# The experts' last step: close() of three of five groups moved from VectorE to GpSimd

## The chip, the cores and the metric

The kernel runs on one core of a Trainium2 chip. Times are device microseconds of one execution of the whole program; the median of 3 runs is 4957.95 us (4957.88 to 4960.18). The profile is of one further execution, taken by the hardware profiler. The core has TensorE (PE, with its weight loads PEld), VectorE (DVE), ScalarE (ACT), GpSimd (POOL) and SyncE (SP), which only issues transfers here. Each engine works through its own queue in order; they meet by semaphores.

## The reference, cut to what matters

A graph layer, a linear attention and a mixture of experts stand one after the other, on 3125 nodes of 256 features, with residuals. Only the last part is touched:

```
def _L0_ffn_ref(x, gate_w, gate_b, w1, b1, w2, b2, gamma, beta):
    gate_logits = x @ gate_w + gate_b
    topk_vals, topk_idx = jax.lax.top_k(gate_logits, K)          # K = 2 of E = 16
    topk_w = jax.nn.softmax(topk_vals, axis=-1)
    h = jax.nn.relu(jnp.einsum('bsh,ehf->bsef', x, w1) + b1)
    expert_out = jnp.einsum('bsef,efh->bseh', h, w2) + b2
    sel = jnp.take_along_axis(expert_out, topk_idx[:, :, :, None], axis=2)
    moe = jnp.sum(topk_w[..., None] * sel, axis=2)
    y = x + moe
    mu = jnp.mean(y, axis=-1, keepdims=True)
    var = jnp.var(y, axis=-1, keepdims=True)
    return (y - mu) / jnp.sqrt(var + EPS) * gamma + beta
...
x = x + _L0_ffn_ref(_layernorm(x, axis=-1)[None], ...)[0]
```

## The kernel before, in words

The program has five stages one behind the other: `prepare` (norm, projections, records of the edges), `pass_one` and `pass_two` (attention over the edges), `finish` (output projection, linear attention, the gate) and `experts`. In the profile `experts` is the last stage. All order within an engine is written out by hand; there is no planner.

In `experts` the 3125 rows stand as 25 blocks (NB) of 128 rows (P) by 256 features (D), and the blocks in five groups of five (G5). Rows sorted by expert go in 66 tiles through the two layers: GpSimd fetches a tile's rows (L2570), TensorE turns and multiplies them, ScalarE applies relu, VectorE adds the second bias (`take`, L2653), GpSimd scatters the result to `back_rows` in DRAM (L2580). While the last scatters run, VectorE adds beta to the residual rows x1 (L2663).

Then comes the end, which the change touches. SP loads the scattered results back, one transfer per group (L2556). For each group g VectorE runs `add_up(g)`: ten scalar_tensor_tensor (L2669), each the sum of xn with a gathered row times its gate weight, then five bn_stats (L2672) and five bn_aggr (L2675). ScalarE takes the square root of the variance (L2603). `scale_of(g)` on VectorE makes reciprocal and shift (L2681, L2682). With these ScalarE writes the normed rows to `second`, five activations (L2606), and raises s_unit. `close(g)` on VectorE multiplies a group of `second` with gamma (L2687) and adds the residual rows x1 (L2688), each one instruction of 128x1280; it raises s_final, on which SP sends the group's rows out (L2561, L2562). In VectorE's queue `close(g - 1)` stands behind `scale_of(g)`, so that ScalarE's activations of a group run beside the next group's sums; the last `close` stands at the end.

`Chain` (`link`) is a helper: an instruction given to it raises a semaphore, and the engine waits for it before it goes on. In the profile's names x1, `second` and the loaded rows are all parts of the tile `big`; gamma, beta, statistics and scales are parts of `WA`.

Of the kernel before, what the change touches and what calls it, by code (L numbers as in the profile page):

```python
# [11 lines left out]
ALU = mybir.AluOpType  # L12
# [6 lines left out]
NB = (N + P - 1) // P  # L19
# [107 lines left out]
def bc(ap, axis, count):  # L127

    shape = list(ap.shape)
    shape.insert(axis, count)  # L130
    return ap.unsqueeze(axis).broadcast_to(shape)


def wait(eng, sem, value):

    if not isinstance(value, int) or value > 0:
        eng.wait_ge(sem, value)
# [1815 lines left out]
G5 = 5  # L1953
# [498 lines left out]
SENT = 3  # L2452
ROWS = 4
FIVES = TOP * NB // G5


def experts(nc, a, dr, kp, sem, out):
# [4 lines left out]
    with ExitStack() as ctx:  # L2462
# [18 lines left out]
        x1, second, W2 = whole(NB, D), whole(NB, D), whole(EXPERTS, FC, D)  # L2481
# [8 lines left out]
        gamma, beta = room(D), room(D)  # L2490
# [19 lines left out]
        s_w = sem("s_w")  # L2510
# [18 lines left out]
        s_unit = sem("s_unit")  # L2529
        s_dve = sem("s_dve")  # L2530
        s_var = sem("s_var")
        s_std = sem("s_std")
        s_final = sem("s_final")
        s_out = sem("s_out")
        block = ctx.enter_context(nc.Block())

        @block.sync
        def _(sp):
            sp.dma_start(b1[:, :], a["L0_ffn_b1"]).then_inc(s_b1, 16)
            sp.dma_start(gamma, a["L0_ffn_gamma"].rearrange("(o e) -> o e", o=1).broadcast_to([P, D])).then_inc(s_w, 16)  # L2540
            sp.dma_start(beta, a["L0_ffn_beta"].rearrange("(o e) -> o e", o=1).broadcast_to([P, D])).then_inc(s_w, 16)
            def load(t):
                i = t % SENT
                e = sp.value_load(tile_ei[0:1, t:t + 1], min_val=0, max_val=EXPERTS - 1)
                wait(sp, s_h, t - SENT + 1)
                sp.dma_start(w1[i], a["L0_ffn_w1"][bass.ds(e, 1), :, :].rearrange("e (c p) f -> p (e c) f", p=P)).then_inc(s_w1[i], 16)
                wait(sp, s_ycopy, t - SENT + 1)
                sp.dma_start(b2row[i], a["L0_ffn_b2"][bass.ds(e, 1), :].broadcast_to([P, D])).then_inc(s_b2[i], 16)

            for t in range(NT):  # L2550
                load(t)
            for i in range(ROWS):
                sp.wait_ge(s_store[i], 16 * len(range(i, NT, ROWS)))
            for g in range(NB // G5):
                rows = back_d[g * G5 * P * TOP:(g + 1) * G5 * P * TOP, :]
                sp.dma_start(back[:, g * G5:(g + 1) * G5, :, :].rearrange("p b c d -> p b (c d)"),  # L2556
                             rows.rearrange("(b p c) d -> p b (c d)", p=P, c=TOP)).then_inc(s_back[g], 16)
            for g in range(NB // G5):
                sp.wait_ge(s_final, g + 1)
                lo, hi = g * G5, min(g * G5 + G5, NB - 1)  # L2560
                sp.dma_start(out[lo * P:hi * P, :].rearrange("(b p) d -> p b d", p=P), second[:, lo:hi, :]).then_inc(s_out, 16)  # L2561
            sp.dma_start(out[(NB - 1) * P:N, :], second[0:LAST, NB - 1, :]).then_inc(s_out, 16)  # L2562
            sp.wait_ge(s_out, 16 * (NB // G5 + 1))

        @block.gpsimd
        def _(pool):
            def fetch(t):
                i = t % ROWS
                wait(pool, s_turned, t - ROWS + 1)
                pool.indirect_dma_start(out=row[i], out_offset=None, in_=x2_d,  # L2570
                                        in_offset=bass.IndirectOffsetOnAxis(ap=come[:, t:t + 1], axis=0)).then_inc(s_row[i], 16)

            pool.wait_ge(s_table, 1)
            for t in range(ROWS):
                fetch(t)
            for t in range(NT):
                if t + ROWS < NT:
                    fetch(t + ROWS)
                pool.wait_ge(s_ycopy, t + 1)
                pool.indirect_dma_start(out=back_d, out_offset=bass.IndirectOffsetOnAxis(ap=go[:, t:t + 1], axis=0),  # L2580
                                        in_=y[t % ROWS], in_offset=None).then_inc(s_store[t % ROWS], 16)

        @block.scalar
        def _(act):
# [25 lines left out]
        def _(dve):  # L2610
            link = Chain(dve, s_dve)
# [10 lines left out]

            for k in range(FIVES):
                u, q = k % 2, slice(k * G5, (k + 1) * G5)
# [10 lines left out]
            link(nc.vector.tensor_scalar(dump, dump, 2.0 * NP + 1, None, ALU.add))  # L2635
            dve.wait_ge(s_slot, FIVES)
            link(nc.vector.tensor_copy(slot, psS[:, 0:NT]))
# [22 lines left out]
                take(t)  # L2660

            dve.wait_ge(s_w, 32)
            link(nc.vector.tensor_tensor(x1, x1, bc(beta, 1, NB), ALU.add))  # L2663

            def add_up(g):
                dve.wait_ge(s_back[g], 16)
                for c in range(TOP):
                    for b in range(g * G5, g * G5 + G5):
                        have = link.post(nc.vector.scalar_tensor_tensor(xn[:, b, :], back[:, b, c, :], share[:, c, b:b + 1], xn[:, b, :], ALU.mult, ALU.add))  # L2669
                    link.until(have)  # L2670
                for i in range(G5):
                    have = link.post(nc.vector.bn_stats(stats[:, i, :], xn[:, g * G5 + i, :]))  # L2672
                link.until(have)
                for i in range(G5):
                    last = nc.vector.bn_aggr(mean_var[:, g * G5 + i, :], stats[:, i, :])  # L2675
                last.then_inc(s_var, 1)

            def scale_of(g):
                blocks = slice(g * G5, g * G5 + G5)
                dve.wait_ge(s_std, g + 1)  # L2680
                link(nc.vector.reciprocal(rstd[:, blocks], rstd[:, blocks]))  # L2681
                nc.vector.scalar_tensor_tensor(shift[:, blocks], mean_var[:, blocks, 0], -1.0, rstd[:, blocks], ALU.mult, ALU.mult).then_inc(s_shift, 1)  # L2682

            def close(g):
                blocks = slice(g * G5, g * G5 + G5)
                dve.wait_ge(s_unit, g + 1)
                link(nc.vector.tensor_tensor(second[:, blocks, :], second[:, blocks, :], bc(gamma, 1, G5), ALU.mult))  # L2687
                nc.vector.tensor_tensor(second[:, blocks, :], second[:, blocks, :], x1[:, blocks, :], ALU.add).then_inc(s_final, 1)  # L2688

            for g in range(NB // G5):  # L2690
                add_up(g)
                scale_of(g)
                if g:
                    close(g - 1)
            close(NB // G5 - 1)

        @block.tensor
        def _(pe):
# [29 lines left out]
            mm.then_inc(s_bT, 1)  # L2728
            for k in range(FIVES):
                pe.wait_ge(s_hots, k + 1)  # L2730
                for i in range(G5):
                    mm = nc.tensor.matmul(psS[:, 0:NT], lo_hot[k % 2][:, i, :], hi_hot[k % 2][:, i, :], start=k + i == 0, stop=k == FIVES - 1 and i == G5 - 1)  # L2732
                mm.then_inc(s_slot, 1)
# [11 lines left out]
def build(nc, a, out):  # L2745
    with ExitStack() as whole:
# [34 lines left out]
        with ExitStack() as edges:  # L2781
# [32 lines left out]
            sem.close()  # L2814
            sem = Sems(nc, "_5")
            experts(nc, a, dr, kp, sem, out)
_INS = ("x", "src", "dst", "edge_attr_5", "node_type_19",
        "L0_gnn_Wk", "L0_gnn_bk", "L0_gnn_Wq", "L0_gnn_bq", "L0_gnn_Wv", "L0_gnn_bv", "L0_gnn_Wa", "L0_gnn_ba",
# [21 lines left out]
```

## Time and profile before

| what | value |
|---|---|
| median of 3 runs | 4957.95 us |
| the profiled execution: its own time, from first to last instruction (span) | 5713.8 us |
| busy in the span: PE, DVE, ACT, POOL | 3201.5, 3637.8, 2345.9, 3354.4 us |
| from 5657 to 5708 us (the groups' work): DVE, ACT, POOL busy | 47.45, 14.34, 0.00 us |
| instructions of POOL in the last 56 us | none |

The profiled execution was longer than the timed ones; no other time of it is given. The shares of the page are means over five stages with different limits; for a change in the last 65 us only the rows of that stretch count. A start and a duration in the timeline are those of the first and of all instructions in a row; an engine's next instruction can start a little before the one ahead of it ends.

### The profile page before, as it was taken

What the parts mean: (1) busy time and instruction counts of PE and PEld (TensorE: products, weight loads), DVE (VectorE), ACT (ScalarE), POOL (GpSimd) and SP (SyncE); (2) the same over time, 40 slices, a digit from 0 to 9 for tenths busy, and PEclk for the clock granted to TensorE, in tenths of its full rate; (3) what the DMA queues carried; (4) which work ended last, traced back from release to release, by engine and by line L of the source; (5) the groups of instructions that cost most, each with busy time, mean ns of one, the idle gap of its engine ahead of it and who ended that gap; (6) DMA issues with size and microseconds to landing.
All of it is one profiled execution on the core that took longest, in us unless ns stands there. A gap on an engine that the chain in (4) does not pass through costs nothing. (4 is left out here: it accounts for less than half of the span.)

```text
span 5713.8 us, 61953 instructions
## 1 busy us (share of the span) xinstructions
PE 3201.5 (56%) x16292; PEld 2177.9 (38%) x16292; DVE 3637.8 (64%) x8152; ACT 2345.9 (41%) x5380; POOL 3354.4 (59%) x3131
## 2 busy tenths in 40 slices
PE   6524444454457555555455555555555489955694
PEld 4312222222224333333333333333433356644694
DVE  7565455555457667766677777766766678966524
ACT  7523333333311444444444444444444367702232
POOL 0366666666620767777667777777777557714352
PEclk9655666666668667766666666666666699977697
DMA  5335566666212666555565555555556578738475
GB/s 149 120 96 156 161 171 178 171 177 171 58 57 72 187 187 186 166 169 175 168 187 178 166 166 167 168 165 165 165 165 163 153 270 301 274 85 261 161 245 180
DMA packets 585990, 965.73 MB, mean 169 GB/s; under 512 B 147041, under 2 KB 387405, under 8 KB 585629
## 3 DMA queue, kind: packets, MB, share of 16 engines
q0 software_dynamic: 151824, 384.84, 22.8%
q1 hardware_dynamic: 333844, 325.84, 20.9%
q10 hardware_dynamic: 99977, 251.09, 12.6%
q8 instruction: 139, 2.28, 0.2%
q14 instruction: 206, 1.69, 0.1%
HBM read 612.82 MB, written 375.69 MB: 173 GB/s over the span
## 5 line engine op out<-in xcount | busy, mean ns | idle before, releaser
L630 POOL DMA_INDIRECT records<-stage,pos x806 | 878.0, 1089 | 702.5 <-DVE stage L908 467.0
L1533 POOL DMA_INDIRECT messages<-stg_a,rec_a x904 | 945.0, 1045 | 481.8 <-issue 263.5
L1525 POOL DMA_INDIRECT kv_a<-kvq_rows,rec_a x904 | 950.1, 1051 | 434.0 <-issue 302.6
L1683 PE MATMUL psA_a<-pay_a,oh_a 128*128 128x260 f32 (+1 forms) x1808 | 811.1, 625 | 0.6 <-ACT wout_a L1554 0.6
L1676 PE MATMUL small_a<-ident,top_a 5*128 5x5 f32 x226 | 57.1, 253 | 1247.4 <-DVE top_a L1654 867.2
L1683 PEld LDWEIGHTS psA_a<-pay_a,oh_a 128*128 128x128 f32 x1808 | 535.5, 310 | 129.7 <-issue 1.3
L680 ACT ACTIVATE rings<-psE 128x512 bf16<-128x512 f32 x496 | 234.0, 516 | 836.0 <-remote 547.0
L1163 PE MATMUL psE<-notyet,identb 128*128 128x512 bf16 x496 | 207.1, 459 | 645.6 <-ACT rings L680 398.0
L1653 DVE TENSOR_TENSOR_SCAN fwd_a<-flag_a,small_a 4x128 f32<-4x128 f32 x226 | 91.1, 403 | 721.7 <-remote 697.2
L1676 PEld LDWEIGHTS small_a<-ident,top_a 5*128 5x128 f32 x226 | 37.3, 165 | 1290.7 <-DVE top_a L1654 888.5
L893 DVE TENSOR_TENSOR pick<-psO,oh 128x510 f32<-128x510 f32 x186 | 114.7, 617 | 641.4 <-remote 473.2
L1554 ACT COPY wout_a<-psA_a 128x265 f32<-128x265 f32 x226 | 86.3, 382 | 758.8 <-DMA types<-in_node_type_dram 379.4
L1791 POOL DMA_INDIRECT part_rows<-wout_b,spot x226 | 293.8, 1300 | 165.0 <-ACT wout_b L1826 105.8
L1163 PEld LDWEIGHTS psE<-notyet,identb 128*128 128x128 bf16 x496 | 51.8, 105 | 730.9 <-ACT rings L680 447.2
L1549 ACT ACT_TABLE_LOAD x225 | 288.7, 1283 | 4.1
L1574 ACT ACT_TABLE_LOAD x225 | 288.7, 1283 | 4.0
L1565 ACT COPY q1s_a<-ctrB_a 128x96 f32<-128x96 f32 x226 | 54.1, 239 | 531.0 <-remote 373.3
L1625 DVE TENSOR_TENSOR prod_a<-kv_a,q1s_a 128x896 f32<-128x896 f32 x226 | 247.3, 1094 | 24.2 <-issue 0.9
L1627 DVE TENSOR_REDUCE att_a<-prod_a 128x16 f32<-128x896 f32 x226 | 245.5, 1086 | 7.7
L1637 DVE TENSOR_TENSOR pay_a<-kv_a,pay_a 128x896 f32<-128x896 f32 x226 | 244.4, 1081 | 0.0
L1933 PE MATMUL psA_b<-msg_b,oh_b 128*128 128x260 f32 x904 | 240.9, 387 | 2.5 <-DVE msg_b L1885 2.2
L1656 DVE TENSOR_REDUCE stg_a<-prod_a 128x16 f32<-128x896 f32 x226 | 236.8, 1048 | 0.0
(506 smaller groups left out, 9209.6 us busy)
## 6 DMA issues: line engine op xcount, KB each, us to landing
messages<-zimg ACTq DMA_DIRECT2D x56, 2080.0 KB
msg_b<-messages ACTq DMA_DIRECT2D x56, 2080.0 KB
win_a<-kvq_rows SPq DMA_DIRECT2D x226, 236.0 KB
WA<-in_L_ffn_w_dram SPq DMA_DIRECT2D x66, 512.0 KB
part_rows<-wout_a SPq DMA_DIRECT2D x226, 132.5 KB
rings<-lo_keys SPq DMA_DIRECT2D x124, 208.0 KB
kv_a<-kvq_rows,rec_a POOLq DMA_INDIRECT x904
messages<-stg_a,rec_a POOLq DMA_INDIRECT x904
```

The costliest lines, as they stand in the source:

```text
L630: pool.indirect_dma_start(out=rec_d, out_offset=bass.IndirectOffsetOnAxis(ap=pos1[:, t:t + 1], axis=0), in_=stage[:, t, :], in_offset=None ...
L1163: nc.tensor.matmul(psE[d][:, 0:n * P], identb[:, :], notyet[:, 0:n, :].rearrange("p b e -> p (b e)"), start=True, stop=False)
L1525: pool.indirect_dma_start(out=kv[u][:, j, :], out_offset=None, in_=kvq_d, in_offset=bass.IndirectOffsetOnAxis(ap=at[:, j, 4:5], axis=0)).t ...
L1533: pool.indirect_dma_start(out=msg_d, out_offset=bass.IndirectOffsetOnAxis(ap=at[:, j, 5:6], axis=0), in_=stg[t % 4][:, j, :], in_offset=No ...
L1549: nc.scalar.activation(pay[t % 2][:, :, 0:HEADS], z[t % 2][:, :, :], ACT.Exp, scale=SCALE).then_inc(s_w, 1)
L1574: nc.scalar.activation(stg[t % 4][:, :, HEADS:HEADS + TD], fr[t % 3][:, :, 2, :], ACT.Sin, scale=turn)
L1625: have_prod = link.post(nc.vector.tensor_tensor(prod[:, :, :, :], k[:, :, 0:VW].rearrange("p s (h d) -> p s h d", h=HEADS), bc(q[:, :, :], ...
L1627: nc.vector.tensor_reduce(att1[:, :, :], prod[:, :, :, :], AX.X, ALU.add).then_inc(s_att1, 1)
L1637: nc.vector.tensor_tensor(v[:, :, HEADS:HEADS + VW].rearrange("p s (h d) -> p s h d", h=HEADS), kv[t % KVS][:, :, PROJ:PROJ + VW].rearrang ...
L1683: mm = nc.tensor.matmul(psA[:, 0:n], oh[t % 2][:, :], pay[t % 2][:, j, 0:n], start=j == 0, stop=j == W - 1)
L1791: pool.indirect_dma_start(out=part_d, out_offset=bass.IndirectOffsetOnAxis(ap=spot[:, t:t + 1], axis=0), in_=wout[u][:, :], in_offset=None ...
L1933: mm = nc.tensor.matmul(psA[t % SUMS][:, 0:MSG], oh[t % HOTS][:, :], msg[q % MSGS][:, i, j, :], start=False, stop=j == 1)
```

## The change

For the first three groups (CLOSED = 25 / 5 - 2 = 3) the two instructions of `close` move to GpSimd, behind its last scatter: it waits for gamma, for the sum of x1 with beta (new semaphore s_xb) and for the group's s_unit; between its product and its sum it waits for the product (s_scaled). VectorE keeps `close` for the last two groups, both now behind all five groups' `add_up` and `scale_of`, and raises s_last for them. SP waits for s_final for three outputs and for s_last for two. The sum of x1 with beta no longer waits for itself; VectorE waits for it before its first `close`.

```diff
--- before.py
+++ after.py
@@ -2452,6 +2452,7 @@
 SENT = 3
 ROWS = 4
 FIVES = TOP * NB // G5
+CLOSED = NB // G5 - 2
 
 
 def experts(nc, a, dr, kp, sem, out):
@@ -2531,6 +2532,9 @@
         s_var = sem("s_var")
         s_std = sem("s_std")
         s_final = sem("s_final")
+        s_xb = sem("s_xb")
+        s_scaled = sem("s_scaled")
+        s_last = sem("s_last")
         s_out = sem("s_out")
         block = ctx.enter_context(nc.Block())
 
@@ -2556,7 +2560,10 @@
                 sp.dma_start(back[:, g * G5:(g + 1) * G5, :, :].rearrange("p b c d -> p b (c d)"),
                              rows.rearrange("(b p c) d -> p b (c d)", p=P, c=TOP)).then_inc(s_back[g], 16)
             for g in range(NB // G5):
-                sp.wait_ge(s_final, g + 1)
+                if g < CLOSED:
+                    sp.wait_ge(s_final, g + 1)
+                else:
+                    sp.wait_ge(s_last, g - CLOSED + 1)
                 lo, hi = g * G5, min(g * G5 + G5, NB - 1)
                 sp.dma_start(out[lo * P:hi * P, :].rearrange("(b p) d -> p b d", p=P), second[:, lo:hi, :]).then_inc(s_out, 16)
             sp.dma_start(out[(NB - 1) * P:N, :], second[0:LAST, NB - 1, :]).then_inc(s_out, 16)
@@ -2579,6 +2586,14 @@
                 pool.wait_ge(s_ycopy, t + 1)
                 pool.indirect_dma_start(out=back_d, out_offset=bass.IndirectOffsetOnAxis(ap=go[:, t:t + 1], axis=0),
                                         in_=y[t % ROWS], in_offset=None).then_inc(s_store[t % ROWS], 16)
+            pool.wait_ge(s_w, 32)
+            pool.wait_ge(s_xb, 1)
+            for g in range(CLOSED):
+                blocks = slice(g * G5, g * G5 + G5)
+                pool.wait_ge(s_unit, g + 1)
+                nc.gpsimd.tensor_tensor(second[:, blocks, :], second[:, blocks, :], bc(gamma, 1, G5), ALU.mult).then_inc(s_scaled, 1)
+                pool.wait_ge(s_scaled, g + 1)
+                nc.gpsimd.tensor_tensor(second[:, blocks, :], second[:, blocks, :], x1[:, blocks, :], ALU.add).then_inc(s_final, 1)
 
         @block.scalar
         def _(act):
@@ -2660,7 +2675,7 @@
                 take(t)
 
             dve.wait_ge(s_w, 32)
-            link(nc.vector.tensor_tensor(x1, x1, bc(beta, 1, NB), ALU.add))
+            nc.vector.tensor_tensor(x1, x1, bc(beta, 1, NB), ALU.add).then_inc(s_xb, 1)
 
             def add_up(g):
                 dve.wait_ge(s_back[g], 16)
@@ -2685,14 +2700,14 @@
                 blocks = slice(g * G5, g * G5 + G5)
                 dve.wait_ge(s_unit, g + 1)
                 link(nc.vector.tensor_tensor(second[:, blocks, :], second[:, blocks, :], bc(gamma, 1, G5), ALU.mult))
-                nc.vector.tensor_tensor(second[:, blocks, :], second[:, blocks, :], x1[:, blocks, :], ALU.add).then_inc(s_final, 1)
+                nc.vector.tensor_tensor(second[:, blocks, :], second[:, blocks, :], x1[:, blocks, :], ALU.add).then_inc(s_last, 1)
 
             for g in range(NB // G5):
                 add_up(g)
                 scale_of(g)
-                if g:
-                    close(g - 1)
-            close(NB // G5 - 1)
+            dve.wait_ge(s_xb, 1)
+            for g in range(CLOSED, NB // G5):
+                close(g)
 
         @block.tensor
         def _(pe):
```

VectorE's queue, the last group and the end of the program, before (`big` with `WA` is the product with gamma, `big` alone the sum with the residual):

```order
L2669 SCALAR_TENSOR_TENSOR xn<-big,share,xn 128x256 x10
L2672 BN_STATS WA<-xn 128x6 x5
L2675 BN_AGGR WA<-WA 128x2 x5
L2681 RECIPROCAL WA<-WA 128x5
L2682 SCALAR_TENSOR_TENSOR WA<-WA 128x5
L2687 TENSOR_TENSOR big<-big,WA 128x1280
L2688 TENSOR_TENSOR big<-big 128x1280
L2687 TENSOR_TENSOR big<-big,WA 128x1280
L2688 TENSOR_TENSOR big<-big 128x1280
L2462 UNCONDITIONAL_BRANCH
```

The groups ahead of it have one pair of L2687 and L2688 each, but for the first, which has none. The same queue after, the last two groups:

```order
L2684 SCALAR_TENSOR_TENSOR xn<-big,share,xn 128x256 x10
L2687 BN_STATS WA<-xn 128x6 x5
L2690 BN_AGGR WA<-WA 128x2 x5
L2696 RECIPROCAL WA<-WA 128x5
L2697 SCALAR_TENSOR_TENSOR WA<-WA 128x5
L2684 SCALAR_TENSOR_TENSOR xn<-big,share,xn 128x256 x10
L2687 BN_STATS WA<-xn 128x6 x5
L2690 BN_AGGR WA<-WA 128x2 x5
L2696 RECIPROCAL WA<-WA 128x5
L2697 SCALAR_TENSOR_TENSOR WA<-WA 128x5
L2702 TENSOR_TENSOR big<-big,WA 128x1280
L2703 TENSOR_TENSOR big<-big 128x1280
```

A second pair of L2702 and L2703 follows and ends the queue; between the groups there is none any more (line numbers are 15 higher in this part of the program). GpSimd's queue at the end of the program, after:

```order
L2577 DMA WA<-x_rows,come_x 128x256
L2587 DMA back_rows<-WA,go_x 6912x256 x5
L2594 TENSOR_TENSOR big<-big,WA 128x1280
L2596 TENSOR_TENSOR big<-big 128x1280
L2594 TENSOR_TENSOR big<-big,WA 128x1280
L2596 TENSOR_TENSOR big<-big 128x1280
L2594 TENSOR_TENSOR big<-big,WA 128x1280
L2596 TENSOR_TENSOR big<-big 128x1280
L2463 UNCONDITIONAL_BRANCH
```

Before, that queue ends with the five scatters; the six tensor_tensor are new there.

## Rows read from the trace of the kernel before

**Rows 1.** The page's first line.
```profile
span 5713.8 us, 61953 instructions
```
**Rows 2.** Chain of waits, 5640 us to the end: start us, us, what.
```profile
5657.20 2.08 DVE xn L2669 x5
...
5664.38 1.99 DVE xn L2669 x5
5666.39 2.08 DVE xn L2669 x5
5668.49 1.74 DVE WA L2672 x5
...
5671.46 1.41 DVE big L2687
5672.90 1.49 DVE big L2688
5674.39 1.99 DVE xn L2669 x5
...
5705.86 1.49 DVE big L2688
```
**Rows 3.** Busy time by engine, one stretch; the columns' line first.
```profile
core 0: us, PE busy (x) PEld busy (x) DVE busy (x) ACT busy (x) POOL busy (x), PEclk, DMA share, GB/s
...
5657.00:5708.00 51.00, 0.00 (x0) 0.00 (x0) 47.45 (x120) 14.34 (x30) 0.00 (x0) 0.50 0.40 147
```
**Rows 4.** Groups, 5640 to 5714 us: busy us, mean ns | idle before, releaser.
```profile
L2669 DVE SCALAR_TENSOR_TENSOR xn<-big,share,xn 128x256 f32<-128x256 f32 x50 | 20.7, 480 | 8.9 <-DMA big<-back_rows 8.7
L2606 ACT ACTIVATE big<-xn,WA 128x256 f32<-128x256 f32 x25 | 12.8, 589 | 2.3 <-DVE WA L2682 2.3
...
L2688 DVE TENSOR_TENSOR big<-big 128x1280 f32<-128x1280 f32 x5 | 7.5, 1492 | 0.2
L2687 DVE TENSOR_TENSOR big<-big,WA 128x1280 f32<-128x1280 f32 x5 | 7.4, 1486 | 0.0
```
**Rows 5.** Timeline at the end: start us, us, instruction [idle before <-releaser].
```profile
5641.63 6.82 DVE L2663 TENSOR_TENSOR big<-big,WA 128x6400 f32<-128x6400 f32 x1
5641.99 7.29 POOL L2580 DMA_INDIRECT back_rows<-WA,go_x  x1 [0.92 <-DVE WA L2653]
...
5664.41 2.57 ACT L2606 ACTIVATE big<-xn,WA 128x256 f32<-128x256 f32 x5 [0.46 <-DVE WA L2682]
```
**Rows 6.** Timeline of VectorE in pass_one, at 3000 and 3289 us.
```profile
2999.66 1.09 DVE L1625 TENSOR_TENSOR prod_a<-kv_a,q1s_a 128x896 f32<-128x896 f32 x1
...
3002.29 1.08 DVE L1637 TENSOR_TENSOR pay_a<-kv_a,pay_a 128x896 f32<-128x896 f32 x1
3003.29 0.29 DVE L1640 SCALAR_TENSOR_TENSOR pay_a<-rec_a,stg_a 128x128 f32<-128x128 f32 x1
...
3005.72 1.05 DVE L1656 TENSOR_REDUCE stg_a<-prod_a 128x16 f32<-128x896 f32 x1
...
3289.38 1.15 DVE L1625 TENSOR_TENSOR prod_a<-kv_a,q1s_a 128x896 f32<-128x896 f32 x1
```
**Rows 7.** GpSimd at the same places; L1625's durations (ns min/median/max).
```profile
2999.72 1.85 POOL L1525 DMA_INDIRECT kv_a<-kvq_rows,rec_a  x1 [0.30 <-issue]
...
3003.18 1.04 POOL L1533 DMA_INDIRECT messages<-stg_a,rec_a  x1 [0.30 <-issue]
...
3005.80 0.96 POOL L1533 DMA_INDIRECT messages<-stg_a,rec_a  x1 [0.31 <-issue]
...
3289.41 0.98 POOL L1533 DMA_INDIRECT messages<-stg_a,rec_a  x1 [0.30 <-issue]
...
L1625 DVE TENSOR_TENSOR prod_a<-kv_a,q1s_a x226: 1091/1093/1148, 1865.3 to 4537.3; 128x896 f32<-128x896 f32 x113
```
**Rows 8.** Groups of GpSimd, 0 to 60 us.
```profile
L605 POOL IOTA low<- 128x128 int32 x2 | 0.4, 225 | 0.4 <-POOLq L2830 0.4
L606 POOL IOTA rings<- 128x256 int32 x1 | 0.3, 332 | 0.0
```

## The prediction

> **What bounds the kernel now.** I read the page's first line [rows 1], then the chain of waits over the last 75 us [rows 2], then the table of engines for the stretch after the experts' loop [rows 3], then the groups and the timeline there [rows 4, 5], and last the one earlier stage in which GpSimd and VectorE work side by side with the same kinds of operands [rows 6, 7]. The diff touches only what follows the experts' loop, some 65 us; the rest is instruction for instruction the same, so I forecast a difference in us.
>
> In that stretch the chain is VectorE almost throughout: ten sums of a gathered row (L2669), five statistics (L2672), the short scale steps, then close(): product with gamma (L2687) and sum with the residual (L2688) [rows 2]. From 5657 to 5708 us VectorE is busy 47.45 of 51 us, ScalarE 14.34, GpSimd 0 [rows 3]. So VectorE's queue sets the end, and GpSimd stands empty. The chain ends with L2688 at 5705.86 + 1.49 = 5707.35; 6.45 us of output transfers follow to the span's end at 5713.8.
>
> The profiled span is 755.9 us longer than the median of 4957.95. The page does not say where those lie. I assume that the end, made of single VectorE instructions, runs alike with and without the profiler, and put the difference worked out here on the median.
>
> **What goes.** close() takes VectorE from 5671.46 to 5674.39, 2.93 us [rows 2]; 1.486 + 1.492 of busy time, slightly overlapped [rows 4]. Before, five of them stand on VectorE, two behind one another at the end. After, two stand there, again behind one another. VectorE loses 3 x 2.93 = 8.8 us. The group without close() is 5671.46 - 5664.38 = 7.08 us. With nothing else changed the last L2688 would end at 5707.35 - 8.8 = 5698.56.
>
> **What stays hidden.** The last two groups' unit rows come from ScalarE: five activations of 0.589 us, 2.6 us after a group's scale [rows 4, 5]; the fourth group's close covers them for the fifth, as before. SP takes the outputs in order, two last ones 2.9 us apart as now, so the 6.45 us behind them stay. The sum with beta loses its own wait: nothing behind it on VectorE reads x1 before the transfers of back rows land, so its cost is nil; its new signal is up some 9 us before the first sums. Behind GpSimd's new waits stand only its own later groups and, on SP, the outputs in order.
>
> **What GpSimd adds.** Six tensor_tensor of 128x1280 with two operands in SBUF. The trace has none on that engine. From below: its IOTA takes 332 ns for 256 elements and 225 for 128 [rows 8], so 0.84 ns an element and 0.12 us fixed; one pass over 1280 elements is 1.19 us. From above: two operands read and one result written one after the other, three passes, 3.3 us; two passes, 2.3. VectorE's own is 1.49. I take 2.8, the middle of two and three passes, as the kind of work nearest to it that this engine shows; the ends go into the range. The Trainium skill (GPSIMD Engine Reference, section 3.1) gives 4497 ns for such an add of 2048 fp32; by proportion an estimate of 2.8 us for 1280, which would leave the sum as it is.
>
> If the engines ran free of each other, GpSimd would need 2 x 2.8 and two gaps of about 0.3, some 6.2 us per group of 7.08: it keeps up, and the saving is the whole 8.8.
>
> **Do they run free of each other?** The earlier stage says no. A GpSimd gather that starts just after VectorE's two-operand product L1625 (2999.66 for 1.09 us) takes 1.85 us in place of about 0.96, ending 0.82 after the product's end [rows 6, 7]. One that starts at 3005.80, under a reduction with one input, takes 0.96. The longest case is in the end itself: a scatter of 7.29 us under the 6.82 us sum with beta [rows 5], again ending 0.83 after it. So while VectorE reads two SBUF tensors, a GpSimd instruction that reads SBUF stands still. The other direction shows too, if faintly: at 3289.38 the product takes 1.15, not 1.09, when a gather starts with it, while the gather keeps its 0.98 [rows 6, 7]; the maximum over all 226 is 1148 ns against a median of 1093 [rows 7]. The gather reads only its indices, so it holds VectorE for some 0.06 us. And GpSimd does get its turn between VectorE instructions that stand in line: the one at 3003.18 ends 0.85 after L1637's end at 3003.37, although the two-operand L1640 had started at 3003.29 [rows 6, 7].
>
> A tensor_tensor on GpSimd reads operands for most of its length. I take it that it holds VectorE's two-operand instructions for all of it. The Trainium skill (SBUF — State Buffer, section "SBUF: two separate sides") states this: the port pair shared by the two engines is an exclusive lock held for the full instruction, and the loser blocks. The trace agrees in one direction with up to 6.8 us, in the other with 0.06 us only.
>
> **Where the six fall.** VectorE ends the scale of a group at 5664.38 and starts the ten L2669 of the next, 4.1 us; they read the gathered row and xn, both in SBUF. ScalarE ends the unit rows at 5664.41 + 2.57 = 5666.98 [rows 5]. So GpSimd's product asks for its turn while the seventh of ten runs, and gets it behind that one; VectorE stands for 2.8. Then one or two L2669 pass in GpSimd's gap (0.30 between its instructions [rows 7], plus the wait for its own product), and the sum takes its turn behind the eighth or ninth: another 2.8. Both land among the L2669, not under the statistics, which have one input. The next group is later by the same shift, so it meets the same place. The cost is 3 x 2 x 2.8 = 16.8, the balance 16.8 - 8.8 = +8.0 us: the last L2688 ends near 5715.4. GpSimd's last sum ends near 5698.7, well ahead of close(3) at 5709.5, so SP's queue does not wait for it. 4957.95 + 8.0 = 4966.0.
>
> **Rivals.**
> 1. *The instruction holds longer.* The same lock, but 3.12 us or more each: (9.9 + 8.8) / 6 = 3.12 is the point from which the kernel is slower by over 0.2%. For: three passes give 3.3, and each handover may cost VectorE something more. Against: two passes give 2.3, and a part of the instruction may not hold anything. At 3.3 the balance is +11.2, 4969.2; at 4.0 it is +15.2, 4973.2. The place is the same run of L2669.
> 2. *No hold worth the name.* GpSimd reads in pieces and lets VectorE through. For: the hold of VectorE that the trace shows is 0.06 us. Against: the 6.82 us hold the other way. Gain the full 8.8: 4949.2, which is 0.18%.
> 3. *One of two is covered.* The sum on GpSimd comes so late (a gap over 1.3 us, three L2669) that it runs under the statistics and scale steps, 2.9 us with hardly a two-operand instruction; or VectorE keeps the turn to the end of its run. Then 3 x 2.8 - 8.8 = -0.4, 4957.6. For: the length fits. Against: 0.30 gaps, and the turn at 3003.18.
>
> **The numbers.** Forecast, with holds of 1.2 to 3.1 (-1.7 to +9.9 by 6 x P - 8.8): 0.40. Rival 1: 0.32. Rival 2: 0.16. Rival 3: 0.12. What a measurement of this kernel can tell from no change is 0.2%, 9.9 us, so faster means under 4948.0, slower over 4967.9. Rival 2 lies 1.1 us inside; I give 0.06 of its 0.16 to faster. Slower is rival 1, 0.32. Same: 0.40 + 0.12 + 0.10 = 0.62. The range takes in rival 2 at 4949.2 and rival 1 up to a hold of 3.7 us (+13.4): 4949 to 4971; the likeliest case alone has 4956 to 4968.
>
> **What would show it.** Right: L2669 in the first four groups' stretch with maxima near 3 us in place of 0.48, two in a group, each under a GpSimd tensor_tensor; the group without close() 12 to 13 us where GpSimd works and 7.1 where it does not; the time from the first L2669 to the last L2688, 50.15 us now, near 58. Rival 2: every L2669 at 0.42 to 0.48 and 41.4 us. Rival 3: one stretched L2669 per group and 49 to 50 us. Rival 1: GpSimd's instruction over 3.1 us. The forecast is wrong altogether if GpSimd's products are stretched rather than VectorE's sums, if its first tensor_tensor starts many us after its unit rows, or if an output waits for GpSimd's last sum.

## The result and the profile after

The changed kernel takes 4973.51 us (4963.68 to 4987.27, 7 runs), the kernel before 4957.88 us in the runs beside it (4951.79 to 4962.59, 7 runs). The ratio is 1.004, interval 1.003 to 1.005: slower, by 15 to 25 us, with 0.2% (9.9 us) as the least that can be told from no change. Ratio and interval come from all the runs; the two medians alone are 15.6 us apart. Forecast were 4966 and a range of 4949 to 4971, so the time lies above the range.

The end of the program went nearly as the prediction's likeliest case said. This is the timeline of the changed kernel (start us, us, instruction, how often; line numbers are 15 higher than before; L2684 answers to L2669, L2594 and L2596 are GpSimd's new product and sum):

```profile
4921.92 4.17 DVE L2684 SCALAR_TENSOR_TENSOR xn<-big,share,xn 128x256 f32<-128x256 f32 x10 [8.86 <-DMA big<-back_rows]
4926.12 1.73 DVE L2687 BATCH_NORM_STATS2 WA<-xn 128x6 f32<-128x256 f32 x5
...
4929.01 9.44 DVE L2684 SCALAR_TENSOR_TENSOR xn<-big,share,xn 128x256 f32<-128x256 f32 x10
4929.13 2.57 ACT L2621 ACTIVATE big<-xn,WA 128x256 f32<-128x256 f32 x5 [0.46 <-DVE WA L2697]
4931.87 2.88 POOL L2594 TENSOR_TENSOR big<-big,WA 128x1280 f32<-128x1280 f32 x1 [17.97 <-ACT big L2621]
4934.84 2.93 POOL L2596 TENSOR_TENSOR big<-big 128x1280 f32<-128x1280 f32 x1
...
4966.02 4.17 DVE L2684 SCALAR_TENSOR_TENSOR xn<-big,share,xn 128x256 f32<-128x256 f32 x10
...
4977.56 1.49 DVE L2703 TENSOR_TENSOR big<-big 128x1280 f32<-128x1280 f32 x1
```

The ten sums of a group take 4.17 us where GpSimd is idle (the first group and the last) and 9.44 us where GpSimd's product and sum run. Single durations show who pays (ns min/median/max):

```profile
L2684 DVE SCALAR_TENSOR_TENSOR xn<-big,share,xn x50: 472/480/3129, 4921.9 to 4969.7; 128x256 f32<-128x256 f32 x50
```

The median stays at 480, the mean of before [rows 4]; the longest is 3129. In the timeline cut to single instructions, the first GpSimd group holds the eighth and the ninth of ten:

```profile
4931.90 3.13 DVE L2684 SCALAR_TENSOR_TENSOR xn<-big,share,xn 128x256 f32<-128x256 f32 x1
...
4934.95 3.10 DVE L2684 SCALAR_TENSOR_TENSOR xn<-big,share,xn 128x256 f32<-128x256 f32 x1
```

They start 0.03 and 0.11 us after GpSimd's product and sum and end 0.28 after each. GpSimd's sum starts 0.09 us after its product's end, and no whole sum of VectorE passes between the two. VectorE shows as busy while it stands, so its busy time hides the wait. From the first sum to the last the stretch of 50.15 us [rows 2] is now 57.15, in the window with the engines' columns as in [rows 3]:

```profile
4921.90:4979.05 57.15, 0.00 (x0) 0.00 (x0) 54.54 (x114) 14.33 (x30) 17.59 (x6) 0.50 0.36 131
```

VectorE has six instructions fewer (114) and 7.09 us more of busy time. So the end cost 7.0 us. The rest of the slowdown, 8 to 18 us, is not in it.

### The profile page after: what moved, and what is told of

It is laid out like the page before. It is cut to its first block and busy times, and to the rows that moved or that the text cites. A ratio compares the mean times of both kernels' runs of the same rounds, so it can differ in the third digit from the quotient of the medians.

```text
span 4985.4 us, 61954 instructions
## 1 busy us (share of the span) xinstructions
PE 3173.4 (64%) x16292; PEld 2176.4 (44%) x16292; DVE 3640.1 (73%) x8146; ACT 2330.6 (47%) x5380; POOL 3329.5 (67%) x3137
## 5 line engine op out<-in xcount | busy, mean ns | idle before, releaser
L630 POOL DMA_INDIRECT records<-stage,pos x806 | 872.6, 1083 | 451.5 <-issue 245.4
L1533 POOL DMA_INDIRECT messages<-stg_a,rec_a x904 | 947.0, 1048 | 275.4 <-issue 251.0
L1525 POOL DMA_INDIRECT kv_a<-kvq_rows,rec_a x904 | 912.2, 1009 | 288.2 <-issue 275.3
L1683 PE MATMUL psA_a<-pay_a,oh_a 128*128 128x260 f32 (+1 forms) x1808 | 843.4, 646 | 0.6 <-ACT wout_a L1554 0.6
L1683 PEld LDWEIGHTS psA_a<-pay_a,oh_a 128*128 128x128 f32 x1808 | 560.2, 325 | 138.3 <-issue 1.2
L1625 DVE TENSOR_TENSOR prod_a<-kv_a,q1s_a 128x896 f32<-128x896 f32 x226 | 247.8, 1097 | 465.6 <-ACT kv_a L1577 463.6
L1577 ACT ACTIVATE kv_a<-fr_a 128x128 f32<-128x128 f32 x226 | 69.8, 309 | 776.0 <-DMA kv_a<-kvq_rows,rec_a 776.0
L1791 POOL DMA_INDIRECT part_rows<-wout_b,spot x226 | 290.4, 1285 | 167.4 <-ACT wout_b L1826 110.1
L1163 PE MATMUL psE<-notyet,identb 128*128 128x512 bf16 x496 | 187.6, 420 | 265.9 <-ACT rings L680 251.5
L1820 ACT ACTIVATE msg_b<-msg_b 128x56 f32<-128x56 f32 x904 | 234.4, 331 | 4.6
L1673 PE MATMUL small_a<-ident,rm_a 128*4 128x128 f32 x226 | 66.9, 296 | 251.8 <-DVE rm_a L1632 250.9
L1704 PE MATMUL psP_a<-wbig,lT_a 25*128 25x384 f32 x452 | 210.5, 546 | 0.0
```

What stands on the lines that cost most here:

```text
L630: pool.indirect_dma_start(out=rec_d, out_offset=bass.IndirectOffsetOnAxis(ap=pos1[:, t:t + 1], axis=0), in_=stage[:, t, :], in_offset=None ...
L1525: pool.indirect_dma_start(out=kv[u][:, j, :], out_offset=None, in_=kvq_d, in_offset=bass.IndirectOffsetOnAxis(ap=at[:, j, 4:5], axis=0)).t ...
L1533: pool.indirect_dma_start(out=msg_d, out_offset=bass.IndirectOffsetOnAxis(ap=at[:, j, 5:6], axis=0), in_=stg[t % 4][:, j, :], in_offset=No ...
L1625: have_prod = link.post(nc.vector.tensor_tensor(prod[:, :, :, :], k[:, :, 0:VW].rearrange("p s (h d) -> p s h d", h=HEADS), bc(q[:, :, :], ...
L1683: mm = nc.tensor.matmul(psA[:, 0:n], oh[t % 2][:, :], pay[t % 2][:, j, 0:n], start=j == 0, stop=j == W - 1)
L1791: pool.indirect_dma_start(out=part_d, out_offset=bass.IndirectOffsetOnAxis(ap=spot[:, t:t + 1], axis=0), in_=wout[u][:, :], in_offset=None ...
```

## The experiments

Behind each ratio stand 5 to 12 runs of the kernel named and 25 or 29 of the kernel before beside them, on the same chip; the tiny copy ran once. In what follows, the end is the stretch from the first sum's start to the end of the last close on VectorE, 50.15 us before.

**The kernel before, again.** No edit.

> The kernel before, unchanged, as a control. Every theory expects 4957.9 us within 3 us and a ratio of 1.000 within 0.001. Its profile should have 50.15 us from the first L2669 to the end of the last L2688, as the first profile had. If the ratio is off by 0.002 or more, the part of the change's 15.6 us that its end does not show (about 8.6 us) can be scatter between runs.

Measured: 4952.48 us against 4955.0, ratio 0.9998 (0.9987 to 1.0009). Both times are lower than the 4957.9 expected; only the ratio counts. Its profiled execution has a span of 4942.5 us, against 5713.8 in [rows 1]; the end is the same to the hundredth:

```profile
4885.90:4936.05 50.15, 0.00 (x0) 0.00 (x0) 47.45 (x120) 14.33 (x30) 0.00 (x0) 0.50 0.40 147
```

So the first profile was not stretched in the end, where the prediction's sums come from. It was ahead of it: from the first to the last start of L1525 in `pass_one` it has 2667.0 us, this one 2361.9. The comparison can tell 0.1%.

**The kernel after, again.** No edit.

> The kernel after, unchanged, on the same chip as the control. Theory A, the hold alone: the end is 57.1 us in place of 50.15 (as in its first profile), so the kernel is 7.0 us slower, 4965, ratio 1.0014; the first comparison's 15.6 us then had 8.6 us of scatter in it. Theory B, the change costs something ahead of the end as well: again 12 to 18 us slower, ratio 1.0025 to 1.0036.

Measured: 4973.95 us, ratio 1.0049 (1.0034 to 1.0064), some 17 to 32 us; 57.12 us from the first sum to the end of the last. Theory A falls: 7.0 us of hold are there again, and some 10 to 25 us more which the end does not contain. The interval reaches over the 18 us that theory B named, but B is the one that stands.

**The order without GpSimd.** The change's queue order and semaphores, the arithmetic all on VectorE.

```diff
-            pool.wait_ge(s_w, 32)
-            pool.wait_ge(s_xb, 1)
-            for g in range(CLOSED):
...
-                nc.gpsimd.tensor_tensor(second[:, blocks, :], second[:, blocks, :], x1[:, blocks, :], ALU.add).then_inc(s_final, 1)
...
-                nc.vector.tensor_tensor(second[:, blocks, :], second[:, blocks, :], x1[:, blocks, :], ALU.add).then_inc(s_last, 1)
+                nc.vector.tensor_tensor(second[:, blocks, :], second[:, blocks, :], x1[:, blocks, :], ALU.add).then_inc(s_final if g < CLOSED else s_last, 1)
...
-            for g in range(CLOSED, NB // G5):
+            for g in range(NB // G5):
                 close(g)
```

> The order and the three semaphores of the change, but all five pairs of product and sum on VectorE, behind all groups' sums; GpSimd has none. Theory A, the hold: 50.1 us from the first sum to the last, time as before, 4958 within 3. Theory B1, semaphores or the shifted program text cost 8.6 us ahead of the end: 4966 to 4967. Theory B2, GpSimd's new instructions cost it: 4958 as in A. Rival for the end, that the order of VectorE's queue and not GpSimd lengthens it: 57 us there and 4965.

Measured: 4953.03 us, ratio 0.9997 (0.9985 to 1.0009), and the end, in the columns of [rows 3]:

```profile
4894.81:4944.96 50.15, 0.00 (x0) 0.00 (x0) 47.44 (x120) 14.32 (x30) 0.00 (x0) 0.50 0.41 151
```

Order, VectorE's and SP's semaphores and shifted program text cost nothing that this comparison can tell, in the end or ahead of it. Both costs come with what this run leaves out: GpSimd's six instructions and its waits ahead of them.

**GpSimd beside the statistics.** Two groups on GpSimd (CLOSED = 2); each of its instructions also waits for the count (sums, kept in VectorE's part) that the tenth sum of a later group raises: the product of group 0 for group 1, its sum for group 2, and so on. For this GpSimd's whole part stands behind VectorE's in the program text; cut to what is new in it:

```diff
-CLOSED = NB // G5 - 2
+CLOSED = 2
...
+                pool.wait_ge(s_dve, sums[2 * g + 1])
                 nc.gpsimd.tensor_tensor(second[:, blocks, :], second[:, blocks, :], bc(gamma, 1, G5), ALU.mult).then_inc(s_scaled, 1)
                 pool.wait_ge(s_scaled, g + 1)
+                pool.wait_ge(s_dve, sums[2 * g + 2])
                 nc.gpsimd.tensor_tensor(second[:, blocks, :], second[:, blocks, :], x1[:, blocks, :], ALU.add).then_inc(s_final, 1)
```

> GpSimd makes product and sum for two groups of five, and each of its four instructions waits until VectorE has ended the ten sums of a group, so that it runs beside the statistics, which read one tensor. Theory A, exclusive hold by instructions with two operands in SBUF: no sum is stretched (0.48 us each), two pairs of 2.93 us leave VectorE, the short two-operand shift step is held 0.1 to 0.4 us in four groups: the end is 44.3 to 46 us in place of 50.15, time 4952 to 4954. Rival, that a GpSimd instruction slows whatever VectorE runs: five statistics of 1.73 us become 4 or more, the end 50 us or longer, 4958 or more. Theory B2 adds 8.6 us to either.

Its timeline (L2661 the sums, L2665 the statistics, L2675 the shift step, L2714 GpSimd's product):

```profile
4916.35 4.17 DVE L2661 SCALAR_TENSOR_TENSOR xn<-big,share,xn 128x256 f32<-128x256 f32 x10
...
4920.55 1.73 DVE L2665 BATCH_NORM_STATS2 WA<-xn 128x6 f32<-128x256 f32 x5
4920.69 2.88 POOL L2714 TENSOR_TENSOR big<-big,WA 128x1280 f32<-128x1280 f32 x1 [19.55 <-DVE xn L2661]
...
4923.35 0.25 DVE L2675 SCALAR_TENSOR_TENSOR WA<-WA 128x5 f32<-128x5 f32 x1
4923.52 4.16 DVE L2661 SCALAR_TENSOR_TENSOR xn<-big,share,xn 128x256 f32<-128x256 f32 x10
```

The end, in the columns of [rows 3]:

```profile
4909.26:4953.77 44.51, 0.00 (x0) 0.00 (x0) 41.88 (x116) 14.32 (x30) 11.53 (x4) 0.50 0.46 167
```

The same GpSimd instruction of 2.88 us leaves the one-input statistics at 1.73 us and the sums at 4.17; only the little two-operand shift step waits, 0.25 for 0.17. The end is 44.51 us, 5.64 less than before. So GpSimd work as such does not hold VectorE: in these runs the hold falls on VectorE's instructions with two operands in SBUF, and those with one keep their time. Yet the kernel takes 4960.93 us, ratio 1.0015 (1.0004 to 1.0025): 2 to 12 us slower with an end that is 5.6 us faster. The second cost is here too, without the hold on the sums.

Where it sits can be read in GpSimd's indirect DMAs (its gathers and scatters), 1100 to 4700 us ahead of the change. First the kernel before (the run called again), then the kernel after; columns are ns min/median/max and first and last start:

```profile
L630 POOL DMA_INDIRECT records<-stage,pos x806: 954/959/6868, 209.3 to 1352.3; - x162
...
L1525 POOL DMA_INDIRECT kv_a<-kvq_rows,rec_a x904: 942/961/1882, 1399.4 to 3761.3; - x181
L1533 POOL DMA_INDIRECT messages<-stg_a,rec_a x904: 956/975/2246, 1419.6 to 3782.3; - x181
...
L1791 POOL DMA_INDIRECT part_rows<-wout_b,spot x226: 982/1367/1935, 3816.6 to 4240.1; - x113
```

```profile
L630 POOL DMA_INDIRECT records<-stage,pos x806: 963/967/6799, 207.9 to 1359.5; - x162
...
L1525 POOL DMA_INDIRECT kv_a<-kvq_rows,rec_a x904: 949/967/1897, 1408.2 to 3795.9; - x181
L1533 POOL DMA_INDIRECT messages<-stg_a,rec_a x904: 965/984/2230, 1429.0 to 3817.1; - x181
...
L1791 POOL DMA_INDIRECT part_rows<-wout_b,spot x226: 982/1367/2105, 3852.1 to 4274.9; - x113
```

Minimum and median are 6 to 9 ns longer at each of the first three; L1791, the only one with a bounds check, keeps both. The stretched first profile lies in between, with medians of 962, 963 and 978, so it is not used here. A step of 6 to 9 ns looks like nothing, but in `pass_one` GpSimd's queue is full. The window of that stage in the kernel before (run again; the fifth pair of numbers is GpSimd):

```profile
1400.00:3785.00 2385.00, 1485.30 (x4293) 1009.53 (x4293) 1870.45 (x4528) 1225.70 (x2483) 1832.60 (x1808) 0.67 0.65 193
```

1832.6 us busy and 1808 gaps of 0.30 [rows 7] make 2375 of 2385 us. So 904 x 6 + 904 x 9 ns = 13.6 us should come straight on top, an estimate from the medians. The next runs ask what brings it.

**One tiny tensor_tensor.** The kernel before, with one instruction more on GpSimd behind its last scatter.

```diff
+        spare = sb("spare", [P, 4])
...
+            pool.wait_ge(s_w, 32)
+            nc.gpsimd.tensor_tensor(spare[:, 0:2], gamma[:, 0:2], gamma[:, 2:4], ALU.add)
```

> The kernel before, with one GpSimd tensor_tensor of 128x2 into a spare tile, behind the last scatter, which nothing waits for. In the profiles with tensor_tensor on GpSimd every indirect DMA of the program, also those that run some 3500 us ahead of it, had medians 7 to 9 ns longer (L1525 967 in place of 961, L1533 984 in place of 975, L630 967 in place of 959). Theory P, presence: the one small instruction brings the whole of it: 967, 984, 967 and 10 to 14 us more time, 4965 to 4969; the end stays at 50.15 us. Theory W, the work of the large ones or what they leave in memory: medians as before, 4955 within 3.

Measured: 4968.15 us against 4951.4, ratio 1.003 (1.0018 to 1.0042), 9 to 21 us, 14.9 in the middle. The instruction itself takes 0.2 us, and the end is 50.15 us, from the timeline and in the columns of [rows 3]:

```profile
4899.77 0.20 POOL L2584 TENSOR_TENSOR spare_x<-WA 128x2 f32<-128x2 f32 x1
...
4907.40:4957.55 50.15, 0.00 (x0) 0.00 (x0) 47.46 (x120) 14.32 (x30) 0.00 (x0) 0.50 0.41 150
```

The indirect DMAs:

```profile
L630 POOL DMA_INDIRECT records<-stage,pos x806: 963/967/6552, 207.9 to 1356.7; - x162
...
L1525 POOL DMA_INDIRECT kv_a<-kvq_rows,rec_a x904: 949/967/1848, 1404.2 to 3778.1; - x181
L1533 POOL DMA_INDIRECT messages<-stg_a,rec_a x904: 965/984/2230, 1425.2 to 3799.3; - x181
```

These are the medians of the kernel after, to the nanosecond. (The expectation speaks of every indirect DMA and of 7 to 9 ns; at L1525 it is 6, and L1791 has no step.) Presence, not work: theory P. One thing comes with the instruction, a wait of GpSimd for gamma (s_w): every run with the longer medians has it behind the last scatter, none without them has, and no run has the wait alone. GpSimd waits for semaphores from start to end in every kernel here, so the wait is the less likely of the two; it is not ruled out. That the 14.9 us are the longer indirect DMAs is argued from the sum of 13.6 us above, and the lengths of the stages, further down, bear it out; no run took the one without the other.

**Six memsets.** The kernel before, with six instructions of a kind that GpSimd has already.

```diff
+        spare = sb("spare", [P, 6])
...
+            for k in range(6):
+                nc.gpsimd.memset(spare[:, k:k + 1], float(k))
```

> The kernel before, with six memsets of one column each on GpSimd behind the last scatter, a kind of instruction that the program has there already. Theory P, a kind of instruction that is new on GpSimd: medians of the indirect DMAs as before (961, 975, 959) and 4955 us within 3. Rival, that any further instructions in GpSimd's queue (their number, or the shift of what follows) lengthen the indirect DMAs: 967, 984, 967 and 4965 to 4969.

Measured: 4956.49 us against 4951.4, ratio 1.0004 (0.9992 to 1.0015), and

```profile
L1525 POOL DMA_INDIRECT kv_a<-kvq_rows,rec_a x904: 942/960/1902, 1404.2 to 3774.5; - x181
L1533 POOL DMA_INDIRECT messages<-stg_a,rec_a x904: 956/975/2244, 1424.8 to 3795.6; - x181
```

The number of instructions is not it, nor the spare tile.

**One tiny copy.** A copy in the place of the tiny tensor_tensor, run once.

```diff
-            nc.gpsimd.tensor_tensor(spare[:, 0:2], gamma[:, 0:2], gamma[:, 2:4], ALU.add)
+            nc.gpsimd.tensor_copy(spare[:, 0:2], gamma[:, 0:2])
```

> As with one small tensor_tensor, but the one instruction is a GpSimd copy of 128x2, also a kind that the program has nowhere else. If any new kind lengthens the indirect DMAs: medians 967 (L1525), 984 (L1533), 967 (L630). If it is tensor_tensor: 961, 975, 959 as before. One look, so the time itself decides nothing here.

```profile
L1525 POOL DMA_INDIRECT kv_a<-kvq_rows,rec_a x904: 947/967/2141, 1405.1 to 3773.8; - x181
L1533 POOL DMA_INDIRECT messages<-stg_a,rec_a x904: 965/984/2227, 1426.1 to 3794.7; - x181
```

The same step, so it is not tensor_tensor alone. (Its single time was 4960.91 us beside 4949.2; it is the only profile from its chip.) What stays open is why. Both kinds read a tile, memset and iota do not; whether that, or a kind being new to the program, or the wait that comes with both, makes the difference, and whether the instruction must run at all, was not tried.

**The sum with beta later.** The kernel before; the other direction of the hold, from the row of 7.29 us in [rows 5].

```diff
             dve.wait_ge(s_w, 32)
+            for i in range(ROWS):
+                dve.wait_ge(s_store[i], 16 * len(range(i, NT, ROWS)))
             link(nc.vector.tensor_tensor(x1, x1, bc(beta, 1, NB), ALU.add))
```

> The kernel before, but VectorE starts the sum with beta (128x6400, two operands in SBUF, 6.82 us) only when the last scatter has landed. Theory of the hold: the last scatter takes about 1 us in place of 7.3, lands some 6.3 us earlier, and the loads of the result start as much earlier; the sum with beta then runs beside the first load and ends within 0.5 us of its landing: 5.5 to 6.3 us less from the start of the last scatter to the first L2669, 4949 in place of 4955, ratio 0.9988. Rival, that the last scatter is long for another reason (it is the last, or waits for memory): still 7 us, and the sum with beta then comes on top, 5 to 7 us more, 4961.

```profile
4880.31 0.96 POOL L2580 DMA_INDIRECT back_rows<-WA,go_x  x1 [0.92 <-DVE WA L2653]
4882.78 7.55 SPq L2556 DMA_DIRECT2D big<-back_rows  x5
4882.90 6.83 DVE L2665 TENSOR_TENSOR big<-big,WA 128x6400 f32<-128x6400 f32 x1 [2.86 <-DMA back_rows<-WA,go_x]
4889.76 2.59 DVE L2671 SCALAR_TENSOR_TENSOR xn<-big,share,xn 128x256 f32<-128x256 f32 x6
```

The last scatter takes 0.96 us in place of 7.29, and 9.45 us pass from its start to the first sum in place of 5657.20 - 5641.99 = 15.21 [rows 2, 5]: 5.8 us less, as expected. Measured: 4940.7 us against 4951.4, ratio 0.9981 (0.9971 to 0.9991), 4 to 14 us less. (The last fence line is cut by its window; all ten sums take 4.17.) This version, without any arithmetic on GpSimd, is faster than the kernel before, and so than the kernel after.

## Why the prediction was wrong

The step that failed is the first: "the rest is instruction for instruction the same, so I forecast a difference in us". It put what the change does ahead of the end at nothing, for no other reason than that the instructions are the same, and gave no rival for it. Their number and order are the same, their durations are not. The kernel before with the small tensor_tensor (and its wait) alone costs 14.9 us (9 to 21). With the 7.0 us of the end that makes 21.9; measured were 20 (15 to 25) in the first comparison and 24 (17 to 32) in the second. GpSimd beside the statistics gives -5.6 + 14.9 = +9.3, measured +7.4 (2 to 12). No rival of mine had this cost; rival 1 had the right side, slower, by a longer hold, and the hold was shorter than forecast.

Where the cost sits can be read from the lengths of the stages. From the first to the last start of L1525 pass 2361.9, 2362.2, 2370.3 and 2360.4 us in the four profiles without the longer medians (before again, order only, six memsets, beta later), and 2387.7, 2371.6, 2377.9, 2373.9 and 2368.7 in the five with them (after, after again, beside the statistics, tiny tensor_tensor, tiny copy). The lines not shown so far are these of order only, beta later, after again and beside the statistics:

```profile
L1525 POOL DMA_INDIRECT kv_a<-kvq_rows,rec_a x904: 942/960/1852, 1403.7 to 3765.9; - x181
L1525 POOL DMA_INDIRECT kv_a<-kvq_rows,rec_a x904: 942/961/1886, 1405.0 to 3765.4; - x181
L1525 POOL DMA_INDIRECT kv_a<-kvq_rows,rec_a x904: 949/967/1883, 1409.9 to 3781.5; - x181
L1525 POOL DMA_INDIRECT kv_a<-kvq_rows,rec_a x904: 947/967/1903, 1400.9 to 3778.8; - x181
```

The second group takes 12.3 us more in the mean, though one profile of each kind overlaps; GpSimd's busy time on L1525 and L1533 grows by as much, from 1835.1 to 1847.4. From the first to the last L630 in `prepare` the mean grows by 3.1 us, from 1146.7 to 1149.7, less than its 806 x 8 ns would give. Together these make 15.4 us. Why the indirect DMAs are longer stays open.

The steps on the end held:

- Three pairs of 2.93 us leave VectorE, 8.8 us. Shown for two of the three: with two groups moved and no hold on the sums the end is 5.64 us shorter, 2 x 2.93 less the little waits of the shift step.
- GpSimd's instruction: 2.8 us from the middle of two and three passes, measured 2.88 to 2.96. The middle was a choice between two bounds and not worked out, so there is some luck in it.
- The Trainium skill's rule (SBUF — State Buffer, section "SBUF: two separate sides") is that the shared port pair is an exclusive lock. The runs agree now in both directions, with 3129 ns for a sum that takes 480 and 7.29 us for a scatter that takes 0.96.
- Both instructions of a group fall among the sums: 9.44 - 4.17 = 5.27 us in the first of three groups, 0.03 less in the others. The term was a little too large: 2.63 us held per instruction, not 2.8. 6 x 2.63 - 8.8 = 7.0, not 8.0. The one or two sums that were to pass between the two did not: GpSimd's gap is 0.09 us, not 0.30, and the sums held are the eighth and the ninth. This changed nothing in the cost.
- ScalarE's activations, the output queue and the 6.45 us of last transfers (6.35 after) stayed hidden or unchanged. GpSimd's last sum, started at 4959.48 with 2.94 us, ended 10.7 us ahead of VectorE's first close at 4973.10.
- Rivals 2 and 3, no hold and one of two covered, did not occur in this kernel; the experiment beside the statistics brought about rival 3's cover for all of GpSimd's instructions.

The change was also forecast to be too small to tell (0.62). That failed for the same reason as the time: the end alone, 7.0 us, would have been inside 0.2%.

## What to carry to other kernels

Before elementwise work goes from VectorE to GpSimd, look at what VectorE runs in that moment: two-operand instructions on both engines take turns, and VectorE then waits for a GpSimd instruction that is nearly twice as long as its own (2.88 against 1.49 us). A kind of instruction that an engine has not run so far can have a price in places which the diff does not touch; compare the median duration of the engine's other instructions, which shows a step of 0.6 to 0.9% in one profile where single times scatter by 25 us. Both profiles must have run alike for this: the stretched one here would have hidden a third of the step. And where VectorE's long two-operand instruction stands beside a GpSimd DMA on the critical path, move the long one.

## What the runs showed of the hardware

- One GpSimd tensor_tensor or copy of 128x2 (with its wait), 0.2 us long and behind the last scatter, makes indirect DMAs throughout the program longer: medians 961 to 967, 975 to 984, 959 to 967 ns at the three lines with the most. L1791, with a bounds check, keeps 982 (its shortest) and 1367. All four profiles with tensor_tensor, and the one with the copy, have the step; four without (before again, order only, six memsets, beta later) do not, and the stretched first profile lies in between. The cause is open.
- VectorE's busy time contains the time in which it stands for GpSimd: 54.54 of 57.15 us busy with six instructions fewer.
- A GpSimd instruction gets its turn between VectorE's two-operand instructions although these follow one another without a gap, twice in a run of ten.
